# A quantised feed-forward with a convolution, written anew: blocks of 456 tokens, row steps multiplied in PSUM

## What is computed

```
def act_quant(x):
    scale = 127.0 / jnp.clip(jnp.max(jnp.abs(x), axis=-1, keepdims=True), 1e-05)
    return jnp.clip(jnp.round(x * scale), -128, 127) / scale
...
h = bit_linear(x, w1)
h = depthwise_conv1d(h.transpose(0, 2, 1), conv_w, conv_b)
h = h.transpose(0, 2, 1)
h = jax.nn.silu(h)
return bit_linear(h, w2)
```

## Time and profile before

| | |
|---|---|
| median of 3 runs | 4590.92 us (4590.12 to 4599.56) |
| profiled execution, own time | 4593.92 us |
| its span | 4592.3 us |
| granted TensorE clock, mean | 0.808 |
| PE / PEld busy | 3408.0 us (74%) / 2285.9 (50%) |
| DVE busy | 3367.0 us (73%) |
| ACT busy | 2281.6 us (50%) |
| POOL busy | 1597.7 us (35%) |
| the changed stage | from 3957.6 us to the end |

### The profile page before, as it was taken

The page is one execution under the profiler, slowest core; times in us unless marked ns, Lnnn a source line. Parts: engine busy times, 40 slices in busy tenths (PEclk is TensorE's granted clock), DMA queues, the critical chain, the costliest instruction groups (busy, mean ns, idle before and its releaser), DMA issues. The chain is left out here.

```text
span 4592.3 us, 59148 instructions
## 1 busy us (share of the span) xinstructions
PE 3408.0 (74%) x17328; PEld 2285.9 (50%) x17328; DVE 3367.0 (73%) x9024; ACT 2281.6 (50%) x3229; POOL 1597.7 (35%) x1578
## 2 busy tenths in 40 slices
PE   5566678888888888675757777489999999344445
PEld 3343445555555455433645555367777777222322
DVE  4499898999899999757889997234444443688887
ACT  1385578888887878622323333133333333455553
POOL 1032333444344433523550100113333332355555
PEclk8666767777777777787988999789999999666667
DMA  5200000000000000042212333444433333201111
GB/s 200 81 7 5 9 8 9 11 11 9 9 8 13 9 9 9 8 187 74 64 32 61 95 85 85 137 131 137 127 124 124 122 108 115 69 26 35 33 34 38
DMA packets 266541, 281.93 MB, mean 61 GB/s; under 512 B 61192, under 2 KB 187276, under 8 KB 265229
## 3 DMA queue, kind: packets, MB, share of 16 engines
q1 hardware_dynamic: 247226, 250.77, 18.0%
q10 hardware_dynamic: 15700, 15.42, 1.0%
q0 software_dynamic: 3328, 12.58, 0.7%
HBM read 213.70 MB, written 65.02 MB: 61 GB/s over the span
## 5 line engine op out<-in xcount | busy, mean ns | idle before, releaser
L643 PE MATMUL score<-KT,q 64*128 64x512 f32 (+1 forms) x1792 | 663.8, 516 | 288.7 <-ACT S L505 144.3
L405 DVE MAX8 cand<-S 128x8 f32<-128x100 f32 (+1 forms) x4096 | 680.8, 258 | 102.4 <-ACT S L505 65.7
L643 PEld LDWEIGHTS score<-KT,q 64*128 64x128 f32 x1792 | 425.3, 258 | 518.3 <-ACT S L505 264.9
L668 PE MATMUL up<-ctx,attnT 128*128 128x384 f32 (+1 forms) x1664 | 613.1, 517 | 0.0
L505 ACT ACTIVATE S<-score 128x1024 f32<-128x1024 f32 (+1 forms) x512 | 409.8, 832 | 122.8 <-PE score L643 122.8
L410 DVE SCALAR_TENSOR_TENSOR S<-S,tops,E 128x3202 f32<-128x3202 f32 x128 | 452.5, 3561 | 6.5 <-ACT E L532 6.5
L668 PEld LDWEIGHTS up<-ctx,attnT 128*128 128x128 f32 (+1 forms) x1664 | 324.3, 205 | 209.1 <-issue 53.0
L2090 DVE TENSOR_TENSOR ff_gelu<-ff_whole,ff_gelu 128x512 fp32r<-128x512 f32 x128 | 97.3, 760 | 429.5 <-ACT ff_gelu L2207 429.5
L514 ACT ACTIVATE E<-S,below 128x3202 bf16<-128x3202 f32 x128 | 379.7, 2967 | 28.0 <-issue 13.3
L532 ACT ACTIVATE E<-S,ebias 128x3202 f32<-128x3202 f32 x128 | 380.2, 2971 | 10.3 <-POOL ebias L362 10.0
L372 POOL TENSOR_TENSOR S<-S 128x512 f32<-128x512 f32 (+1 forms) x224 | 252.4, 1166 | 301.1 <-DVE S L410 300.9
(11 more groups left out here) (371 smaller groups left out, 6725.6 us busy)
## 6 DMA issues: line engine op xcount, KB each, us to landing
s_hankel<-scratch_K SPq DMA_DIRECT2D x128, 256.0 KB, 4.5
ff_w_low<-scratch_w1l SPq DMA_DIRECT2D x112, 256.0 KB, 2.6
ff_w_low<-scratch_w2l SPq DMA_DIRECT2D x112, 256.0 KB, 2.7
x_in<-in_x SPq DMA_DIRECT2D x8, 1024.0 KB, 6.8
scratch_xt<-xt_prep POOLq DMA_DIRECT2D x8, 1024.0 KB, 8.7
q<-scratch_qt SPq DMA_DIRECT2D x128, 64.0 KB, 1.9
X<-in_L_ffn_w SPq DMA_DIRECT2D x2, 4096.0 KB, 25.4
mod_xt<-scratch_xt SPq DMA_DIRECT2D x32, 256.0 KB, 2.7
```

Of the source, the lines that this page charges most:

```text
L405: nc.vector.max(cand[:, h, 8 * k:8 * k + 8], S[:, b, h, k * SEG:end])
L643: last = nc.tensor.matmul(score[k % 2][:, j % 2, 0:w], lhsT=q[at, part, h // 2, :], rhs=KT[at, h // 2, chunk(j)], start=(part == 0), stop= ...
L668: last = nc.tensor.matmul(up[:, 0:DV], lhsT=attnT[0:w, e, c - 4 * g, :], rhs=ctx[0:w, c, :], start=(c == 0), stop=(c == GC - 1))
```

## The change

`bit_feed_forward` is written anew. All loops are written out.

- Blocks are of STEP = 456 tokens, four rows of 114 (the last block has 448, four rows of 112): nine blocks instead of 16, and still eight steps each.
- `hp` has a ring of three tiles. `dequantise` multiplies in place, in PSUM; `hidden` and `others` are gone. ScalarE reads tap 0 for both groups from PSUM, and VectorE adds taps 1 and 2 for both groups, 456 tokens each, from PSUM. GpSimd adds no taps.
- The largest value: ScalarE's `measure` writes the absolute values of each step's `g` to `size`; VectorE's `raise_high` keeps a running maximum in `high`, and behind the last step a maximum over the two groups in `top`.
- `scaling` stays on GpSimd, and `quantise` moves there from VectorE; in the last block both are shared with VectorE (`quantise_last`).
- `op` is one bank. A second product for 114 tokens (16 products in a row) is followed by `finish` of that row, written into `x2`, which is stored.
- The transposed maxima and the spread steps share one bank.

The core of the diff:

```
+    ROWS = 114
+    STEP = QUAD * ROWS
+    BLOCKS = -(-T // STEP)
+    RING = 3
+    LAG = 4
+    SHARED = 2
+        hp = [ps(f"bf_hp{k}", [P, 2, BANK]) for k in range(RING)]
+        op = ps("bf_op", [P, BANK])
...
+                def quantise(n, j):
+
+                    pool.wait_ge(s["scaled"], JC * n + j + 1)
+                    if n >= 2:
+                        pool.wait_ge(s["second_done"], QUAD * (n - 1))
+                    nc.gpsimd.tensor_scalar(gq[:, n % 2, 2 * j:2 * j + 2, 0:QUAD * rows(n)], part(n, j), ROUND, ROUND,
+                                            ALU.add, ALU.subtract).then_inc(s["quantised"], 1)
...
+                    dve.wait_ge(s["first_done"], JC * n + j + 1)
+                    v.tensor_tensor(at, at, rowstep[:, STEP * n:STEP * n + w].unsqueeze(1).broadcast_to([P, 2, w]), ALU.mult).then_inc(s["dequantised"], 1)
...
+                    dve.wait_ge(s["tapped0"], JC * n + j + 1)
                     for k in range(1, 3):
+                        dve.drain()
+                        for e in range(2):
+                            f = 2 * j + e
+                            to = conv[:, j % DEEP, e, 0:w]
+                            last = v.scalar_tensor_tensor(to, hp[(JC * n + j) % RING][:, e, k:k + w], taps[:, f, k:k + 1], to, ALU.mult, ALU.add)
                     last.then_inc(s["tapped"], 1)
...
+                    elif j:
+                        v.tensor_tensor(high[:, :, 0:w], size[:, j % DEEP, :, 0:w], high[:, :, 0:w], ALU.max).then_inc(s["raised"], 1)
+                    if j == JC - 1:
+                        dve.drain()
+                        v.tensor_tensor(top[:, 0:w], high[:, 0, 0:w], high[:, 1, 0:w], ALU.max).then_inc(s["top_done"], 1)
...
+                    dve.wait_ge(s["second_done"], QUAD * n + k + 1)
+                    v.scalar_tensor_tensor(x2[0:r, n % 2, k], op[0:r, :], undo[0:r, n % 4, k:k + 1], x2[0:r, n % 2, k],
+                                           ALU.mult, ALU.add).then_inc(s["y_ready"], 1)
...
+                for n in range(BLOCKS + 3):
                     for j in range(JC):
+                        if j > LAG and 2 <= n <= BLOCKS + 1:
+                            finish(n - 2, j - LAG - 1)
+                        if j == 0 and n >= 3:
+                            finish(n - 3, QUAD - 1)
+                        if n < BLOCKS:
+                            if j + 1 < JC:
+                                dequantise(n, j + 1)
+                            elif n + 1 < BLOCKS:
+                                dequantise(n + 1, 0)
+                            add_taps(n, j)
+                        if j and n < BLOCKS:
+                            raise_high(n, j - 1)
+                        if j == 0 and 1 <= n <= BLOCKS:
+                            raise_high(n - 1, JC - 1)
+                        if j == 2 and 1 <= n <= BLOCKS:
+                            steps(n - 1)
+                        if j == LAG and n == BLOCKS:
+                            quantise_last(n - 1)
...
+                    if QUAD * n + k:
+                        pe.wait_ge(s["y_ready"], QUAD * n + k)
+                    for f in range(FC):
+                        last = nc.tensor.matmul(op[0:r, :], lhsT=gq[:, n % 2, f, r * k:r * (k + 1)], rhs=W2q[:, f, :], start=(f == 0), stop=(f == FC - 1))
+                    last.then_inc(s["second_done"], 1)
+
+                for n in range(BLOCKS + 2):
                     for j in range(JC):
+                        if n < BLOCKS:
+                            first(n, j)
+                        if j == 1 and 1 <= n <= BLOCKS:
+                            turn_top(n - 1)
+                        if j == 3 and 1 <= n <= BLOCKS:
+                            spread_steps(n - 1)
+                        if j >= LAG and n >= 2:
+                            second(n - 2, j - LAG)
```

More of the change, by code:

```diff
@@ L2471, in _ @@
[L2471 to L2482, removed]
-                for b in range(2):
-                    store(half - 2, b)
-                    load_x(half - 1, b)
@@ L2491, in _ @@
+                for n in range(BLOCKS - 2, BLOCKS):
+                    store(n)
+                for b in range(2):
+                    sp.wait_ge(s[f"stored{b}"], 16 * ((BLOCKS + 1 - b) // 2))
             @block.gpsimd
             def _(pool):
[L2493 to L2501, removed]
@@ L2520, in _ @@
[L2520 to L2529, removed]
+                nc.gpsimd.memset(every[:], 1.0).then_inc(s["set"], 1)
@@ L2621, in _ @@
-                half = BLOCKS // 2
-                for n in range(4):
-                    turn(n // 2, n % 2, ends=n)
-                with dve.Fori(0, half - 2) as i:
-                    turn(i + 2, 0)
-                    turn(i + 2, 1)
-                largest(half - 1, 1, 0)
-                largest(half - 1, 1, 1)
-                steps(half - 1, 1)
-                for j in range(JC):
-                    quantise(half - 1, 0, j)
-                finish(half - 2, 1)
-                dve.drain()
@@ new lines, in steps @@
+                def steps(n):
+                    r = rows(n)
+                    dve.wait_ge(s["top_turned"], n + 1)
+                    v.tensor_reduce(most[0:r], mp[0:r], AX.X, ALU.max)
+                    dve.drain()
+                    v.tensor_scalar(most[0:r], most[0:r], LEAST, None, ALU.max)
+                    dve.drain()
+                    v.reciprocal(step[0:r], most[0:r])
+                    v.tensor_scalar(undo[0:r, n % 4], most[0:r], mean[0:r, 1:2], 1.0 / LEVEL, ALU.mult, ALU.mult)
+                    dve.drain()
+                    v.tensor_scalar(step[0:r], step[0:r], LEVEL, None, ALU.mult)
+                    dve.drain()
+                    for k in range(QUAD):
+                        last = v.tensor_scalar(diag[0:r, r * k:r * (k + 1)], const["ident"][0:r, 0:r], step[0:r, k:k + 1], None, ALU.mult)
+                    last.then_inc(s["steps_ready"], 1)
@@ L2730, in turn @@
-                def turn(m, b, ends=3):
-                    for j in range(JC):
-                        first(m, b, j)
-                        if ends > 2 and 2 <= j < 6:
-                            second(*before(m - 1, b), j - 2)
-                        if ends and j == 6:
-                            turn_top(*before(m, b))
-                        if ends and j == JC - 1:
-                            spread_steps(*before(m, b))
-                    pe.drain()
-                    pe.sem_inc(s["block_done"], 1)
```

344 lines of the change are left out of this document (140 added, 204 removed).

## The result

The changed kernel takes 4671.56 us (median of 4 runs, 4665.73 to 4673.05), the kernel before 4592.14 us beside it on the same chip: a ratio of 1.0168, 95% interval 1.015 to 1.0185. It is slower by 1.7%, and 55 us faster than forecast. The profiled execution has a span of 4669.0 us and a mean granted clock of 0.812.

A forecast was written before the change was run, and what follows sets the result against it. VectorE's instruction stream was taken as the bound. Start 8.4, block 0 40, block 1 57.6, blocks 2 to 8 600.4 and tail 64 made 770.4 us, 135.7 above 634.7, hence 4727 us; range 4600 to 4790.

The forecast's parts named there:

- plain step: VectorE's work for 256 hidden channels of a block, dequantise, taps, raising high and drains: 5.00 us, eight per block.
- rival 4: In dequantise: writing the result to PSUM doubles its time, 79 us more, 4806 us in all; chance 0.05.
- D: Steps 5, 6 and 7: VectorE stands still for 16 + 8 products after finish, 8.1 us, three times a block.
- Rival 1: The wait D isn't there, TensorE being ahead when finish is done: 170 us less, 4557 us; chance 0.13.
- Rival 2: TensorE's granted clock is 2.4 GHz in all these waits: D 5.3 us, 4630 us in all; chance 0.14.
- Rival 3: TensorE's clock stays at 1.2 GHz: D 10.2 us, 44 us more, 4771 us in all; chance 0.10.
- cold start: In D, TensorE begins at the lower clock after idling: 2.35 to 3.5 us lost on top of 5.2.
- tail: End of the stage, from the last finish and quantising through seven second-product turns to the store: together 64 us.
- port waits: VectorE operations with two SBUF inputs held by GpSimd, beside five of eight raise_high: 1.1 us each, 5.5 a block.
- A: Stall before dequantise 2, behind turn_top's transposes and eight first products in TensorE's queue: 4.5 us a block.
- steps: The chain of steps on VectorE, outside the plain steps: 2.7 us a block, taken as unchanged from before.
- B: Stall before dequantise 4, where spread_steps waits for the end of steps, plus eight products: 5.3 us a block.

The follow-up runs named there:

- experiment 1: The changed kernel with each first product issued one step earlier in TensorE's queue, in every step: 4469.23 us, ratio 0.9727 to the kernel before.
- experiment 2: The changed kernel with first products issued one step earlier only in steps 4 to 7, where second products stand: 4532.42 us, ratio 0.9868 to the kernel before.
- experiment 4: The changed kernel in its own order, with op in two banks and the hp ring cut from three to two: 4579.96 us, ratio 0.9968 to the kernel before.
- experiment 5: The changed kernel with 24 unread products ahead of each second product that waits, except in the last two blocks: 4626.75 us, ratio 1.0072 to the kernel before.
- experiment 7: On top of experiment 1, GpSimd's rounding replaced by times 1.0 plus 0.0, rounding left out: 4463.7 us, ratio 0.9719 to the kernel before.
- experiment 9: The changed kernel with GpSimd's scaling replaced by adding and subtracting 1.0, so all its work is TENSOR_SCALAR: 4669.2 us, ratio 1.0168 to the kernel before.
- experiment 6: The changed kernel with GpSimd's rounding replaced by times 1.0 plus 0.0, rounding left out: 4668.32 us, ratio 1.0162 to the kernel before.
- experiment 8: On top of experiment 1, rounding split: GpSimd multiplies by 1.0 and adds ROUND, ScalarE subtracts it: 4459.81 us, ratio 0.9708 to the kernel before.

## Why the prediction came out as it did

**The plain step was right.** Forecast 5.00 us; in block 0 `dequantise` starts at 3979.59, 3984.57 and 3989.55, 4.98 apart.

```profile
L2526 DVE TENSOR_TENSOR bf_hp<-bf_hp,rowstep x72: 1096/1121/1121, 3964.9 to 4592.3; 128x916 f32<-128x916 f32 x64, 128x900 f32<-128x900 f32 x8
L2548 DVE TENSOR_TENSOR bf_high<-bf_size,bf_high x54: 1092/1109/3003, 3983.5 to 4605.6; 128x912 f32<-128x912 f32 x48, 128x896 f32<-128x896 f32 x6
L2505 POOL TENSOR_SCALAR bf_gq<-bf_silu x66: 3245/3256/4197, 4040.0 to 4623.1; 128x912 bf16<-128x912 f32 x64, 128x896 bf16<-128x896 f32 x2
L2497 POOL TENSOR_TENSOR bf_silu<-bf_silu,bf_scale x66: 2097/2109/2975, 4035.8 to 4616.6; 128x912 f32<-128x912 f32 x64, 128x896 f32<-128x896 f32 x2
```

`dequantise` takes 1.12 us (forecast 1.11): writing to PSUM costs nothing that shows, and rival 4 is out. The rounding takes 3.26 us (forecast 3.2, from the row of 7.13 us for 2048), the scaling 2.11 (2.2). The Trainium skill (GPSIMD Engine Reference, Engine selection) has one-input work at about line rate, an estimate of 0.8 us for the rounding; the row of 3.26 us disagrees for this pair of operations, as the dearer of the two rows did.

**D was right in place and cause, and nearly in size.** Forecast 8.1 us, 21 times, 170 us; measured 8.05, 7.81 and 7.87 in the block shown, 8.31, 7.65 and 7.78 in the one before, and 7.75 on average over 20 waits, 155.0 us. The 21st was a slip of the count: the last block's third `finish` has no `dequantise` behind it. Rival 1 (no D) holds only when the order or the bank is changed (experiments 1, 2 and 4). Rivals 2 and 3 put D at 5.3 or 10.2: the first is what experiment 5 gets, the second was never seen (the longest is 8.31). Of the forecast's two bounds for the cold start, 2.35 and 3.5 us, the lower one fits: D is on average 2.4 us above the 5.31 of experiment 5.

**Where 55 us were over-forecast.** By the spans it is 59 us: the profiled execution before lay 3.0 us above its median, the one after 0.9 below. Blocks 2 to 7 took 79.1 us on average where 86.0 was forecast, 41.6 us in all. The first and the last block together are 12.6 too long in the forecast, 8 of it the third D of the last block; block 1 is 3.9, the start 1.1. The tail was forecast at 64 us and took 64.2. All these errors but the tail's have one sign, so the direction was right by its mechanism and not by errors that cancel. The terms of a block, in the one shown (78.46, so 7.5 less than 86.0):

| term | forecast | measured |
|---|---|---|
| port waits | 5.5 | 0.45 |
| maxima, one too many | 8 x 1.11 | 7 x 1.11 |
| A | 4.5 | 3.7 |
| D, three | 24.3 | 23.7 |
| steps | 2.7 | 2.5 |
| B | 5.3 | 5.0 |

They make 5.05 + 1.1 + 0.8 + 0.6 + 0.2 + 0.3 = 8.1. Three small waits that the forecast had not (0.16, 0.16 and 0.45 us) stand against them, which leaves 7.3 of the 7.5. The port waits differ from block to block: L2548 has (1.361 - 1.109) x 54 = 13.6 us of them, 1.7 a block over eight blocks.

The term that was furthest off is this one: "beside five of the eight `raise_high`", 1.1 us each, which is about 40 held maxima. In the trace 29 began beside GpSimd's work, and they were held 0.47 us on average: 16 beside the product of two tensors 0.68, 13 beside the slow rounding 0.21. So it had two errors. It priced any GpSimd instruction beside a maximum as a hold, while the slow rounding, which fills 230.4 of GpSimd's 370.8 us, holds only in its first 0.8 us. And it took VectorE to be working through GpSimd's 43 us, while VectorE stands still in D for a good part of them. The Trainium skill's form (SBUF — State Buffer, Who interferes with whom), a wait for the whole instruction, gave the estimate of 7 us a block and was further off; for TENSOR_TENSOR on GpSimd the runs agree with it to 0.14 to 0.17 us, and for the slow TENSOR_SCALAR they do not (0.8 of 3.25 us). The count of eight was a slip too: the block's first step has nothing to raise.

**The new bound.** With D gone, the forecast's own terms give 46.4 us for a block without waits (40 + 3.0 + 0.7 + 2.7); experiment 1 has 49.04. GpSimd is busy for 47.76 and VectorE for 46.04 of it, both nearly full. The same stretch of experiment 7 stands below it:

```profile
4162.62:4211.66 49.04, 32.51 (x134) 16.38 (x134) 46.04 (x62) 25.79 (x33) 47.76 (x17) 0.88 0.14 48
```

```profile
4162.62:4211.66 49.04, 32.88 (x133) 16.47 (x131) 45.73 (x61) 25.80 (x33) 27.52 (x16) 0.86 0.14 48
```

There GpSimd works for 27.52 us only, VectorE for 45.73, and the last six full blocks take 49.3 us on average, as in experiment 1. So VectorE's work, the holds in its maxima with it, is the bound there, and not GpSimd's.

## What to carry to other kernels

Where one engine both frees the accumulator and consumes another product of the same in-order queue, look at what stands behind the wait: put independent work ahead of the waiting instruction before making any instruction faster. A single bank is enough only if the queue's order covers its turn; each such wait costs more when the idle time also lowers TensorE's clock (7.75 in place of 5.3 us here). Price contention between engines by the pair of instructions that really meet, only for the time in which both are running, and count how often they meet. Where a stage is compared between runs, take its own stretch of the trace: here the stages ahead of it moved its start by 10 us.

## What was not expected of the hardware

- The slow TENSOR_SCALAR on GpSimd (add, subtract; 3.26 us for 912 elements) holds a two-input VectorE instruction only in its first 0.8 us, and gets longer itself: 3.35 us on average in experiment 9, 3.89 in experiment 1. The fast form (multiply, add) takes 1.15 us on average in experiment 6 (median 0.95); in experiments 6 to 8 only six maxima began beside it, too few to say how long it holds. All 78 that began beside the product of two tensors there were held, by 1.05 us on average.
- Unread products ahead of a wait took 2.4 us off the average wait of 7.75, and the granted clock of the products behind it was 1.00 where it had been 0.50.
